# Two transformer layers with routed experts: results of the first experts stored at their tokens' places, and sums and values kept on chip

## The chip, the cores and the metric

The kernel runs on one core of a Trainium2 chip, as one program. The metric is the device time of one execution in microseconds; the number shown for a kernel is the median of its runs. All data are float32.

## The reference

Four sequences of 1024 tokens (4096 rows) of width 256 pass through four blocks, each with a layer norm in front and a residual around it. The functions, cut to what is computed:

```python
x = L0_attn_x                                   # (4, 1024, 256)
x = x + L0_attn(layernorm(x))                   # x W_in -> silu * sigmoid; A, B, C = x W_A, x W_B, x W_C (N = 16)
                                                # state = state * exp(A) + x B; out = sum(state * C); rms norm; W_out
x = x + L0_ffn(layernorm(x))                    # 8 experts, top 2 of softmax(x gate_w + gate_b)
                                                # expert e: relu(x w1[e] + b1[e]) w2[e] + b2[e], hidden 512
x = x + L1_attn(layernorm(x))                   # below
x = x + L1_ffn(layernorm(x))                    # shared: silu(x Sg) * (x Su) Sd, FS = 256
                                                # + top 2 of 16: silu(x Wg[e]) * (x Wu[e]) Wd[e], F = 128

def L1_attn(x):                                 # 16 heads of 16
    Q, K, V = split(x @ W_qkv.T)
    Q, K = rope(Q), rope(K)                     # x0 cos - x1 sin, x0 sin + x1 cos, on even and odd columns
    scores = where(causal, Q K^T / 4, -inf)
    return softmax(scores) V @ W_o.T

def L0_ffn(x):
    topk_vals, topk_idx = top_k(softmax(x @ gate_w.T + gate_b), 2)
    ...
    return sum(expert_out[topk_idx] * topk_vals)  # two rows per token, weighted
```

## The kernel before

The program is a row of six stages. Each is one block with a list of instructions per engine (SP, which issues DMAs; TensorE; VectorE; ScalarE, called ACT; GpSimd, called POOL), written out by hand, with semaphores between the lists and a barrier between stages. A tile is 128 tokens; there are 32.

**Front** (0 to 421 us): layer norm, gate, scan and output projection, then the router of the first experts, in chunks of four tiles. VectorE writes the normalised rows `r_xn` (L516), one instruction for each tile; it finds for each token and choice the expert (`best_all`, L538) and the position in that expert's region (`pos_f`, L538 to L566). GpSimd sends each tile's rows twice, by indirect stores, into `gathered_dram`, where each expert's rows lie together (L364 to L370). Behind each region lie rows of zeros, stored by SP from `zeros`. At the end VectorE works out the list of tiles to run, and `moved` (L659, L660), the distance between an expert's region and its tiles in the list.

**First experts** (421 to 697 us), `run_wide_experts`: 71 tiles from the list. For each, SP loads 128 gathered rows and the expert's first weights; TensorE turns the rows, multiplies by both weights; VectorE adds biases, ACT applies the relu and, three tiles later, stores the result at row `t * 128` of `outputs_dram` (L1406). In this stage VectorE also makes the table `pos` of places in `outputs_dram` for each token and choice (`settle`, L2733, five instructions).

**Projection** (697 to 860 us), `project_qkv`: 8 groups of 4 tiles. SP loads the rows `x1`; GpSimd fetches, with one indirect load for each tile and choice, the two expert results per token into `d_ye` (L1520 to L1526). VectorE adds them, weighted, to `x` (`add_experts`, L1561 to L1572) and takes mean and variance; GpSimd's power makes `rstd`, VectorE the bias, ACT normalises, TensorE turns the rows and multiplies by the weights: q and k transposed and split into even and odd columns, v plain. VectorE multiplies each of the four halves by the cosine or sine table, giving 8 products a group in `d_by` (`rotate`, L1601). Of the four sums of products, GpSimd makes three (`add_turned`, L1533) and VectorE the last (`last_sum`, L1589). ACT rounds each sum to a number that TensorE multiplies exactly (`hi`), VectorE takes the difference (`lo`, `rest`, L1604, L1606), and both go to `qkt_dram`, `hi` by ACT's queue and `lo` by SP's. The sum `x2` and the values `v` are stored by SP (`store_x2`, `store_v`). The work is pipelined over ticks: at tick t VectorE runs `add_experts(t)`, `rest(t-3)`, `shift(t)`, `last_sum(t-2)`, `rotate(t-1)`.

**Attention** (861 to 1361 us): 32 pairs of heads (8 pairs for each sequence). SP loads q and k for each pair, and v for each sequence (`load_v`, L1862) into `v_raw`; GpSimd spreads v into `t_vs` with a column of ones (`values`, L1924) and zeroes the masked triangle of the exponentials. The last attended pieces are copied out of PSUM by ACT (`t_att`, L1990). At step `4 * NX` of its list ACT issues the load of the second experts' up weights `wgu_sb`, 4.2 MB (`fetch(act)`, L1996; the issue is at L2794).

**Back** (1361 to 1505 us): 16 groups of two tiles. SP loads for each the attended heads, their inverse sums and the residual `x2` (`k_res`, L2189 to L2200), in a ring. VectorE scales the heads (L2276), TensorE multiplies by W_o, VectorE adds the residual (`add_res`, L2278), normalises, and routes; GpSimd sends the rows into the second `gathered_dram` by indirect stores. The down weights of the second experts and the shared ones are fetched by ACT's queue here.

**Second experts and finish** (1505 to 1712 us). In the second experts' loop GpSimd already sends the results to their tokens' places by indirect stores.

Lines of issue that the steps touch:

```python
for tick in range(groups + 2):                     # GpSimd, projection
    if live(tick + 1): gather(tick + 1, range(J // 2))
    if live(tick):     rsqrt(tick)
    if live(tick + 1): gather(tick + 1, range(J // 2, J))
    if live(tick - 2): add_turned(tick - 2, 0); add_turned(tick - 2, 1)
```

## Time and profile before

| | |
|---|---|
| median of 3 runs | 1712.64 us (1706.57 to 1714.9) |
| the profiled execution's own time | 1713.81 us |
| its span | 1712.1 us |
| TensorE busy | 1522.8 us (89%) |
| VectorE busy | 1000.7 us (58%) |
| ACT busy | 734.9 us (43%) |
| GpSimd busy | 575.6 us (34%) |
| DMA | 235.21 MB, mean 137 GB/s |
| front | 0 to 421 us |
| first experts | 421 to 697 us |
| projection | 697 to 861 us |
| attention | 861 to 1361 us |
| back | 1361 to 1505 us |
| second experts | 1505 to 1652 us |
| finish | 1652 to 1712 us |

All come from one profiled execution, but for the median. The busy shares are means over stages of quite different make-up. A stage begins with the first load of its own that SP issues behind the barrier; the bounds are read from those loads and are good to a microsecond or two.

### The profile page before, as it was taken

To read this page: it belongs to the slowest core of one execution; us is meant where nothing else is said; L and a number is where in the kernel's file an instruction comes from. 1 tells how busy PE (TensorE), PEld (TensorE's weight loads), DVE (VectorE), ACT (ScalarE), POOL (GpSimd) and SP (SyncE) were. 2 spreads that over 40 slices of the span, in tenths; PEclk is the share of its full clock that TensorE was granted. 3 is DMA by queue.
4 is the path that set the end of the run, shared out by engine and by line. 5 is a ranking of instruction groups with operands and counts; after the bars stand their busy time and mean duration, and the time that the engine had idled before them with its cause. 6 is when DMAs were issued, how large, how long until landed. Compare 5 with 4: busy or idle time off the path is not lost. (4 is left out here: it accounts for less than half of the span.)

```text
span 1712.1 us, 31150 instructions
## 1 busy us (share of the span) xinstructions
PE 1522.8 (89%) x9903; PEld 1138.2 (66%) x9903; DVE 1000.7 (58%) x3394; ACT 734.9 (43%) x1537; POOL 575.6 (34%) x1009
## 2 busy tenths in 40 slices
PE   6999999982999999588588999999999679579988
PEld 3777777762999999344365666666666468458877
DVE  3344544442332323378877888888888258645558
ACT  3444444420222222233325777776777523234420
POOL 3123333334000000478452323333222227735530
PEclk9999999985999999799889999999999979789999
DMA  7001111113777776478879767667664276755546
GB/s 224 1 25 44 47 47 47 35 50 130 223 207 218 206 216 190 148 226 293 263 115 190 99 93 116 91 92 112 94 94 69 63 227 204 188 134 156 157 154 206
DMA packets 170062, 235.21 MB, mean 137 GB/s; under 512 B 25040, under 2 KB 121936, under 8 KB 169776
## 3 DMA queue, kind: packets, MB, share of 16 engines
q1 hardware_dynamic: 134128, 171.55, 43.4%
q0 software_dynamic: 13008, 35.57, 6.3%
q10 hardware_dynamic: 22768, 26.11, 4.8%
q8 instruction: 84, 1.38, 0.3%
q14 instruction: 74, 0.61, 0.1%
HBM read 147.90 MB, written 84.98 MB: 136 GB/s over the span
## 5 line engine op out<-in xcount | busy, mean ns | idle before, releaser
L1983 ACT ACTIVATE t_probs<-t_ps_st 128x512 f32<-128x512 f32 x576 | 313.1, 596 | 134.9 <-PE t_ps_st L2037 125.4
L1964 DVE CUSTOM_DVE_ANT_0 t_seen<-t_ps_s,t_later 128x512 bf16<-128x512 f32 (+3 forms) x512 | 285.8, 587 | 22.9 <-PE t_ps_s L2023 20.8
L2037 PE MATMUL t_ps_st<-t_qs,t_ks 128*128 128x512 f32 (+3 forms) x768 | 244.0, 367 | 7.3 <-ACT t_probs L1983 5.7
L2023 PE MATMUL t_ps_s<-t_ks,t_qs 96*128 96x512 f32 (+3 forms) x768 | 248.7, 364 | 0.5 <-ACT t_neg_max L1976 0.5
L1936 POOL TENSOR_SCALAR_AFFINE_SELECT t_probs<-t_probs 128x128 f32<-128x128 f32 x512 | 137.3, 300 | 316.3 <-ACT t_probs L1983 314.6
L2037 PEld LDWEIGHTS t_ps_st<-t_qs,t_ks 128*128 128x128 f32 x768 | 137.5, 190 | 81.6 <-ACT t_probs L1983 43.7
L1964 DVE CUSTOM_DVE_ANT_0 t_seen<-t_ps_s,t_later,t_first_max 128x512 bf16<-128x512 f32 (+3 forms) x256 | 140.6, 549 | 50.7 <-PE t_ps_s L2023 50.7
L1524 POOL DMA_INDIRECT d_ye<-outputs_dram,r_pos_all x64 | 64.8, 1013 | 297.2 <-POOLq L1304 279.4
L2053 PE MATMUL t_ps_o<-t_probs,t_vs 128*17 128x256 f32 (+1 forms) x2560 | 155.7, 362 | 0.5 <-issue 0.5
L2023 PEld LDWEIGHTS t_ps_s<-t_ks,t_qs 96*128 96x128 f32 x768 | 139.4, 191 | 18.0 <-DVE t_first_max L1964 1.6
L1345 PE MATMUL m_ps_h<-m_xt,m_w_t 128*128 128x128 f32 x1136 | 140.2, 277 | 0.0
L1345 PEld LDWEIGHTS m_ps_h<-m_xt,m_w_t 128*128 128x128 f32 x1136 | 134.4, 194 | 0.1
L1353 PE MATMUL m_ps_y<-w_sb,m_ht 128*128 x568 | 134.4, 380 | 0.0
L834 PE MATMUL ps_h<-w_in,xnt 128*128 128x512 f32 x256 | 126.4, 619 | 0.6 <-ACT xnt L672 0.6
L1378 DVE TENSOR_TENSOR m_h<-m_ps_h,b_turned 128x512 f32<-128x512 f32 x71 | 49.1, 692 | 132.6 <-PE m_ps_h L1345 132.6
L1404 ACT ACTIVATE m_ht<-m_h 128x512 f32<-128x512 f32 x71 | 44.7, 629 | 160.2 <-DVE m_h L1378 160.2
L1353 PEld LDWEIGHTS m_ps_y<-w_sb,m_ht 128*128 128x128 f32 x568 | 102.5, 190 | 11.3 <-issue 0.3
L2053 PEld LDWEIGHTS t_ps_o<-t_probs,t_vs 128*17 128x17 f32 x2560 | 59.2, 97 | 72.3 <-issue 28.1
L1129 POOL DMA_INDIRECT outputs_dram<-m_y,m_place x79 | 75.8, 959 | 68.3 <-DVE m_place L1217 65.7
L355 POOL TENSOR_TENSOR xi<-xi,sig_z 128x512 f32<-128x512 f32 x32 | 40.6, 1269 | 139.0 <-ACT sig_z L684 138.9
L1157 PE MATMUL m_ps_h<-wgu_sb,m_xt 128*128 x316 | 82.4, 384 | 0.0
L368 POOL DMA_INDIRECT gathered_dram<-r_xn,pos x64 | 63.4, 991 | 54.0 <-DVE pos L565 38.6
(329 smaller groups left out, 2690.6 us busy)
## 6 DMA issues: line engine op xcount, KB each, us to landing
m_w_t<-in_w_dram SPq DMA_DIRECT2D x71, 512.0 KB, 4.1
t_qs<-qkt_dram SPq DMA_DIRECT2D x124, 128.0 KB, 5.8
t_ks<-qkt_dram SPq DMA_DIRECT2D x124, 128.0 KB, 6.0
m_x_t<-gathered_dram SPq DMA_DIRECT2D x79, 128.5 KB, 2.1
m_x_t<-gathered_dram SPq DMA_DIRECT2D x71, 128.0 KB, 3.8
outputs_dram<-m_y ACTq DMA_DIRECT2D x71, 128.0 KB, 4.0
qkt_dram<-d_hi ACTq DMA_DIRECT2D x32, 256.0 KB, 4.5
qkt_dram<-d_lo SPq DMA_DIRECT2D x32, 256.0 KB, 5.6
```

What stands on the lines that cost most here:

```text
L834: last = nc.tensor.matmul(ps_h[h][:], xnt[:, n % 2, j, :], w_in[:, j, h * DI:(h + 1) * DI], start=(j == 0), stop=(j == KD - 1))
L1129: nc.gpsimd.indirect_dma_start(out=outputs[:, :], out_offset=bass.IndirectOffsetOnAxis(ap=place[:, t:t + 1], axis=0), in_=y[:, t % RING, : ...
L1157: last = nc.tensor.matmul(ps_h[t % 2][:], xt[:, t % 2, j, :], w_up[:, j, bass.ts(expert[t], width)], start=(j == 0), stop=(j == KD - 1))
L1345: last = nc.tensor.matmul(ps_h[t % 2][:, f, :], w_t[:, t % WRING, j, f * P:(f + 1) * P], xt[:, t % 2, j, :], start=(j == 0), stop=(j == KD ...
L1353: last = nc.tensor.matmul(ps_y[t % 2][:, 0:DM], ht[:, t % 2, j, :], w_down[:, j, bass.ts(expert[t], DM)], start=(j == 0), stop=(j == block ...
L1524: nc.gpsimd.indirect_dma_start(out=ye[:, g % 2, j, i, :], out_offset=None, in_=outputs[:, :], in_offset=bass.IndirectOffsetOnAxis(ap=kept[ ...
L1936: nc.gpsimd.affine_select(out=diag, in_=diag, compare_op=ALU.is_ge, fill=0.0, base=0, pattern=[[1, P]], channel_multiplier=-1).then_inc(ma ...
L1964: nc.vector.tensor_tensor_reduce(out=seen[:, (NP * p + x) % (RS + 1), 0:keys], in0=bank_of(p, x)[:, 0:keys], in1=masks, scale=1.0, scalar= ...
L1983: nc.scalar.activation(probs[:, p % 2, i // NST, base:base + STC], ps_st[(NX * p + i) % RT][:], ACT.Exp, scale=HD ** -0.5).then_inc(exp_re ...
L2023: nc.tensor.matmul(bank_of(p, x)[:, 0:keys], q[0:MAX_ROW, head, qc * P:(qc + 1) * P], k[0:MAX_ROW, head, k0:k0 + keys], start=True, stop=T ...
L2037: last = nc.tensor.matmul(ps_st[(NX * p + i) % RT][:, col:col + width], k[:, head, kc * P:(kc + 1) * P], q[:, head, q0:q0 + width], start= ...
L2053: last = nc.tensor.matmul(ps_o[32 * g:32 * g + VR, col:col + width], vs[:, (p // PAIRS) % 2, kc, 2 * (p % PAIRS) + head, :], probs[:, p % ...
```

## The change

The rows of the first experts carry, in a 257th column, the place of their token and choice: row `2 * token + choice` of `outputs_dram`. VectorE writes each normalised row twice, once for each choice. After an expert's tile is done, GpSimd sends the result by an indirect store to these rows; rows of filling go to places behind. The projection then loads its two rows a token with a plain DMA, as one piece of 2 KB for each token, and GpSimd's gathers, the `settle` steps and the tables for it go. The sum stays in SBUF for the whole rest of the kernel (`total`); it is also stored, for the first 12 tiles, and loaded again in the back stage, since attention uses that part of `total` for buffers of its own. ACT writes v straight to `t_vs`; the store, load and spreading of v go. GpSimd makes all four sums of the rotation and two of the four differences, VectorE the other two. The load of `wgu_sb` moves from ACT's queue in attention to SP's queue in the back stage, behind the load of group 9. The diff at its core:

```diff
 front
-    r_xn = sb("r_xn", [P, 2, B4, DM])
+    r_xn = sb("r_xn", [P, 2, B4, 2, DM + 1])
+    r_token = sb("r_token", [P, C, B4, 2])
...
             def scatter(u, b):
                 if b == 0:
                     pool.wait_ge(pos_ready, u + 1)
+                    pool.wait_ge(r_placed, u + 1)
...
-                        in_=r_xn[:, u % 2, b, :], in_offset=None).then_inc(scattered[u % 2], 16)
+                        in_=r_xn[:, u % 2, b, i, :], in_offset=None).then_inc(scattered[u % 2], 16)
...
+                    nc.vector.tensor_copy(r_xn[:, r % 2, :, :, DM], r_token[:, r]).then_inc(r_placed, 1)
-                nc.vector.tensor_scalar(r_xn[:, r % 2, b, :], x1[:, r % 2, b, :], r_mean_var[:, b, 0:1],
+                nc.vector.tensor_scalar(r_xn[:, r % 2, b, :, 0:DM], x1[:, r % 2, b, :].unsqueeze(1).broadcast_to([P, 2, DM]), r_mean_var[:, b, 0:1],
...
-                nc.vector.tensor_copy(of_chunk(best_all, r), best_f[:]).then_inc(kept_ready, 1)
...
-                nc.vector.tensor_copy(of_chunk(pos_f_all, u), pos_f[:]).then_inc(kept_ready, 1)
 run_wide_experts
+        def _(pool):
+            def send(t):
+                pool.wait_ge(place_taken, t + 1)
+                pool.wait_ge(y_ready, t + 1)
+                nc.gpsimd.indirect_dma_start(out=outputs[:, :], out_offset=bass.IndirectOffsetOnAxis(ap=place[:, t:t + 1], axis=0),
+                                             in_=y[:, t % RING, :], in_offset=None).then_inc(stored[t % RING], 16)
...
+            def take_place(t):
+                dve.wait_ge(x_loaded[t % RING], 16 * (t // RING) + 16)
+                nc.vector.tensor_tensor(place[:, t:t + 1], x_t[:, t % RING, DM:DM + 1], spare[:, t:t + 1], ALU.min).then_inc(place_taken, 1)
...
             for i in range(n_list + 2):
-                late(dve, i)
                 if live(i - 1):
+                    take_place(i - 1)
                     hide(i - 1)
...
-            def store(t):
-                act.wait_ge(y_ready, t + 1)
-                act.dma_start(outputs[t * P:(t + 1) * P, :], y[:, t % RING, :]).then_inc(stored[t % RING], 16)
 project_qkv, SP
             def load(g):
                 wait(sp, x2_ready, J * (g - 1))
-                sp.dma_start(x_t[:, g % 2], rows(x_dram, g)).then_inc(x_loaded[g % 2], 16)
+                sp.dma_start(total[:, J * g:J * (g + 1), :], rows(x_dram, g)).then_inc(x_loaded[g % 2], 16)
+                sp.dma_start(ye[:, g % 2].rearrange("p j i n -> p j (i n)"),
+                             outputs[2 * g * TG:2 * (g + 1) * TG, :].rearrange("(j p i) n -> p j (i n)", p=P, i=2)).then_inc(ye_loaded[g % 2], 16)
...
-                if live(tick):
-                    store_x2(tick)
+                if tick < SPILL // J:          # SPILL = 12
+                    store_sum(tick)
...
-                if live(tick - 1):
-                    store_v(tick - 1)
 project_qkv, GpSimd
+                nc.gpsimd.tensor_tensor(qk[:, 2 * which + 1, :], by[:, s, which, 2, :], by[:, s, which, 3, :], ALU.add).then_inc(sum_ready, 1)
+            def rest_late(g):
+                for n in range(2, NB):
+                    pool.wait_ge(hi_ready, NB * g + n + 1)
+                    nc.gpsimd.tensor_tensor(lo[:, g % 2, n, :], qk[:, n, :], hi[:, g % 2, n].bitcast(FP32), ALU.subtract).then_inc(lo_late_ready, 1)
...
+            for tick in range(groups + 3):
+                if live(tick - 3):
+                    rest_late(tick - 3)
                 if live(tick):
                     rsqrt(tick)
-                if live(tick + 1):
-                    gather(tick + 1, range(J // 2, J))
 project_qkv, VectorE
                 if live(tick - 3):
-                    for n in range(NB):
+                    for n in range(2):
                         rest(tick - 3, n)
...
-                if live(tick - 2):
-                    last_sum(tick - 2)
 project_qkv, ACT
-                    nc.scalar.activation(v_t[:, g % 2, 2 * h:2 * h + 2, :], ps_v[:, 2 * h:2 * h + 2, :], ACT.Copy).then_inc(v_ready, 1)
+                    nc.scalar.activation(vs[:, g // 2, j:j + 2, :, 0:HD], ps_v[:, 2 * h:2 * h + 2, :].rearrange("p j (h d) -> p j h d", d=HD),
+                                         ACT.Copy).then_inc(v_ready, 1)
 attention
-                if tick % PAIRS == PAIRS // 2 and live(tick + PAIRS // 2):
-                    load_v(tick // PAIRS + 1)
...
-                if tick % PAIRS == PAIRS // 2 + 1 and live(tick + PAIRS // 2):
-                    values(tick // PAIRS + 1)
...
-                if step == 4 * NX:
-                    fetch(act)
+    att = total[:, 0:2 * KD, :].rearrange("p (s k) d -> p s (k d)", s=2)
+    seen = total[:, 2 * KD:2 * KD + RS + 1, :].bitcast(BF16)
 back, SP
-                sp.dma_start(res[:, s], res_dram[g * G * P:(g + 1) * G * P, :].rearrange("(j p) n -> p j n", p=P)).then_inc(x_loaded[s], 16)
+            def load_sum(i, tiles):
+                sp.dma_start(total[:, tiles, :], res_dram.rearrange("(t p) n -> p t n", p=P)[:, tiles, :]).then_inc(sum_loaded[i], 16)
             load(0)
+            load_sum(0, slice(0, 4))
             load(1)
             load(2)
+            load_sum(1, slice(4, SPILL))
...
                 load(g)
+                if g == 9:
+                    fetch_late(sp)             # load_moe1_up: wgu_sb, 4.2 MB
 back, VectorE
-                nc.vector.tensor_tensor(total[:, g * G:(g + 1) * G], res[:, g % R], ps_wo[g % 2][:], ALU.add).then_inc(x_ready, 1)
+                nc.vector.tensor_tensor(these, these, ps_wo[g % 2][:], ALU.add).then_inc(x_ready, 1)
```

## Rows read from the trace of the kernel before

**Rows 1.** Windows, core 0: stretch, length, busy (instructions) of PE, PEld, DVE, ACT, POOL, clock, DMA, GB/s.
```profile
445.00:698.00 253.00, 249.03 (x1727) 231.29 (x1725) 76.05 (x139) 67.13 (x132) 0.34 (x1) 1.00 0.70 200
698.00:860.00 162.00, 112.16 (x336) 63.44 (x336) 113.65 (x250) 54.97 (x104) 107.72 (x96) 0.83 0.78 246
764.00:780.00 16.00, 14.75 (x40) 7.89 (x40) 12.63 (x32) 6.13 (x12) 12.83 (x13) 0.84 0.96 319
860.00:1360.00 500.00, 488.29 (x4194) 318.82 (x4194) 404.70 (x1540) 333.48 (x640) 165.10 (x554) 0.99 0.65 101
1360.00:1500.00 140.00, 98.67 (x516) 81.23 (x516) 91.45 (x402) 42.25 (x74) 78.17 (x92) 0.83 0.72 200
```
**Rows 2.** Timeline, projection: start, us, engine, line, out<-in, xcount [idle before <-releaser].
```profile
733.97 7.11 PE L1711 MATMUL d_ps_qk<-d_xnt,d_w_qk 128*128 128x512 f32 x16 [0.77 <-DVE d_by L1601]
...
777.39 4.87 DVE L1601 TENSOR_TENSOR d_by<-d_ps_qk,d_turn 128x512 f32<-128x512 f32 x8
780.45 7.11 PE L1711 MATMUL d_ps_qk<-d_xnt,d_w_qk 128*128 128x512 f32 x16 [0.77 <-ACT d_xnt L1645]
785.87 1.67 DVE L1568 SCALAR_TENSOR_TENSOR d_part<-d_ye,r_prob_all,d_x 128x256 f32<-128x256 f32 x4 [3.61 <-issue]
787.39 3.62 PE L1718 MATMUL d_ps_v<-w_qkv,d_xnt 128*128 128x256 f32 x16
790.77 0.17 DVE L1581 TENSOR_SCALAR d_var_eps<-d_mean_var 128x4 f32<-128x4 f32 x1
790.85 2.51 DVE L1606 TENSOR_TENSOR d_lo<-d_qk,d_hi 128x512 f32<-128x512 f32 x4
791.02 1.43 POOL L1531 TENSOR_TENSOR d_rstd<-d_var_eps,mhalf 128x4 f32<-128x4 f32 x1 [1.06 <-DVE d_var_eps L1581]
...
830.13 8.97 PE L1711 MATMUL d_ps_qk<-d_xnt,d_w_qk 128*128 128x512 f32 x16 [0.20 <-DVE d_by L1601]
...
860.62 0.34 SPq L1736 DMA_DIRECT2D t_qs<-qkt_dram  x1
```
**Rows 3.** The tile `d_ye`: least/median/longest ns, first to last start; then its DMA.
```profile
L1524 POOL DMA_INDIRECT d_ye<-outputs_dram,r_pos_all x64: 944/958/1485, 697.7 to 812.3; - x64
...
  DMA d_ye<-outputs_dram,r_pos_all: 11.9, 2
```
**Rows 4.** The tile `d_by`: least/median/longest ns, first to last start.
```profile
L1601 DVE TENSOR_TENSOR d_by<-d_ps_qk,d_turn x64: 673/682/691, 730.2 to 841.1; 128x512 f32<-128x512 f32 x64
...
L1538 POOL TENSOR_TENSOR d_qk<-d_by x16: 1257/1282/1788, 749.3 to 846.3; 128x512 f32<-128x512 f32 x16
```
**Rows 5.** Timeline, end of the projection.
```profile
831.74 3.55 DVE L1606 TENSOR_TENSOR d_lo<-d_qk,d_hi 128x512 f32<-128x512 f32 x4
...
833.19 1.55 POOL L1538 TENSOR_TENSOR d_qk<-d_by 128x512 f32<-128x512 f32 x1 [5.03 <-DVE d_lo L1606]
```
**Rows 6.** Timeline of attention, ACT and its queue.
```profile
912.30 0.60 ACT L1990 ACTIVATE t_att<-t_ps_o 128x512 f32<-128x512 f32 x1
...
920.01 6.87 ACTq L2794 DMA_DIRECT2D wgu_sb<-in_w_gu_dram  x1
...
934.31 0.60 ACT L1990 ACTIVATE t_att<-t_ps_o 128x512 f32<-128x512 f32 x1
...
948.80 0.60 ACT L1990 ACTIVATE t_att<-t_ps_o 128x512 f32<-128x512 f32 x1
```
**Rows 7.** Windows, the stretch in which the up weights move (columns as Rows 1).
```profile
932.00:936.00 4.00, 4.00 (x36) 2.93 (x39) 3.32 (x15) 3.30 (x7) 1.87 (x7) 0.89 1.09 347
```
**Rows 8.** Timeline, back stage: SP's queue and VectorE at group 10.
```profile
1417.48 0.46 SPq L2200 DMA_DIRECT2D k_res<-x_dram  x1
...
1433.04 0.68 DVE L2276 TENSOR_TENSOR k_scaled<-k_headst,k_inv_t 128x512 f32<-128x512 f32 x1
```
**Rows 9.** Timeline, front stage, VectorE.
```profile
278.05 0.69 DVE L450 TENSOR_TENSOR xi<-ps_h,sig_a 128x512 f32<-128x512 f32 x1 [1.52 <-ACT sig_a L678]
...
390.56 1.38 DVE L516 TENSOR_SCALAR r_xn<-x,r_mean_var,r_rstd 128x256 f32<-128x256 f32 x4
```

More of the change, by code:

```diff
@@ L1266, with run_wide_experts @@
 WRING = 4
-def run_wide_experts(nc, sb, pb, sem, c, E, gathered, outputs, kept, w1_dram, b1_turned, w_down, b_down, weights, late):
+SPILL = 12
+def run_wide_experts(nc, sb, pb, sem, c, E, gathered, outputs, kept, w1_dram, b1_turned, w_down, b_down, weights):
     ident = c["ident"]
@@ L1323, in _ @@
                 fetch(t)
+        @block.gpsimd
+        def _(pool):
[4 more added lines that the diff above has]
+                                             in_=y[:, t % RING, :], in_offset=None).then_inc(stored[t % RING], 16)
+            nc.gpsimd.iota(spare[:], pattern=[[P, n_list]], base=2 * TOK, channel_multiplier=1,
+                           allow_small_or_imprecise_dtypes=True).then_inc(spare_ready, 1)
+            for t in range(n_list):
+                send(t)
+            for s in range(RING):
+                pool.wait_ge(stored[s], 16 * len(range(s, n_list, RING)))
         @block.tensor
@@ L1519, in _ @@
         def _(pool):
-            def gather(g, tiles):
-                wait(pool, x2_ready, J * (g - 1))
-                for j in tiles:
-                    for i in range(2):
-                        nc.gpsimd.indirect_dma_start(
-                            out=ye[:, g % 2, j, i, :], out_offset=None, in_=outputs[:, :],
-                            in_offset=bass.IndirectOffsetOnAxis(ap=kept["pos"][:, J * g + j, i:i + 1], axis=0)).then_inc(gathered[g % 2], 16)
             def rsqrt(g):
@@ L1637, in normalise @@
                 for j in range(J):
-                    nc.scalar.activation(xn[:, j, :], x2[:, g % 2, j, :], ACT.Identity, bias=bias[:, j:j + 1],
+                    nc.scalar.activation(xn[:, j, :], total[:, J * g + j, :], ACT.Identity, bias=bias[:, j:j + 1],
                                          scale=rstd[:, j:j + 1]).then_inc(xn_ready, 1)
@@ L2700, in build @@
                 phase(front, c, x_in, w_in, w_abc, w_out, norm_w, x1_dram, gate_w, gate_b, gathered[0], kept, E0, fetch)
-                kept.update(here=wsb("r0_here", [P, 2 * NT, E0]), steps=Chain(nc.vector, sem("r0_settled"), 5))
                 phase(run_wide_experts, c, E0, gathered[0], outputs[0], kept, w1, b1_turned, w2_sb, b2_sb,
-                      (moe0_loaded, 16 * (H0 // P + 2)), lambda dve, i: settle(dve, nc, kept, i))
+                      (moe0_loaded, 16 * (H0 // P + 2)))
+            total = whole.enter_context(nc.sbuf_tensor("whole_sum", [P, NT, DM], FP32, side="right"))
+            vs = ahead.enter_context(nc.sbuf_tensor("t_vs", [P, BATCH, TPB, NH, HD + 1], FP32, side="right"))
             q_first, k_first = (ahead.enter_context(nc.sbuf_tensor(n, [P, 2, SEQ], FP32R, side="right")) for n in ("t_qs0", "t_ks0"))
-            phase(project_qkv, c, x1_dram, outputs[0], kept, x2_dram, w_qkv, rope, qkt_dram, v_dram,
+            phase(project_qkv, c, x1_dram, outputs[0], kept, total, x2_dram, w_qkv, rope, qkt_dram, vs,
                   lambda eng: load_heads(eng, 0, q_first, k_first, qkt_dram, first_loaded))
@@ L2714, in build @@
         wsb = lambda n, s, d=FP32: whole.enter_context(nc.sbuf_tensor(n, s, d))
+        phase(attention, c, q_first, k_first, first_loaded, qkt_dram, vs, total, headst_dram, inv_dram)
+        ahead.close()
         wgu_sb = wsb("wgu_sb", [P, KD, E1 * 2 * F1])
-        phase(attention, c, q_first, k_first, first_loaded, qkt_dram, v_dram, headst_dram, inv_dram,
-              lambda eng: load_moe1_up(eng, moe1_loaded, wgu_sb, w_gu))
-        ahead.close()
         wd_sb = wsb("wd_sb", [P, F1 // P, E1 * DM])
```

189 lines of the change are left out of this document (66 added, 123 removed).

## The prediction

> **What bounds the kernel now.** I read the table of engines by stage first. The six stages are separated by barriers, so each has a limit of its own, and only what ends last in a stage counts. In the first experts TensorE is busy 249 of 253 us and in attention 488 of 500, both at full clock: there, work on other engines is free as long as it does not delay TensorE. The projection (698 to 860) is different: no engine is full (TensorE 112, VectorE 114, GpSimd 108 of 162 us), and the DMA share is 0.96 in its middle. The back stage (1360 to 1500) has no full engine either; its DMA share is 0.72 [rows 1].
>
> Then the projection's timeline, one group of four tiles [rows 2]. The matmuls of group 1 start at 733.97 and those of group 7 at 830.13: 16.0 us a group. The reader should see who waits: VectorE sits idle 3.61 us before a group's first sum (785.87), although TensorE and ACT have nothing late. The view of the tile that is gathered says why: 64 indirect loads, 0.96 us each on GpSimd [rows 3]. Eight of them a group with 0.3 us between are 10.1 us, three rotation sums at 1.28 [rows 4] are 3.8, the power 1.4: 15.3 of the 16.0. GpSimd sets the pace, with DMA close behind.
>
> **The projection after.** Out of GpSimd's list: all 64 gathers. Into it: one sum (1.28) and two differences (1.28 each) a group, so 6 x 1.28 + 1.4 = 9.1 us. Out of VectorE's: one sum and two differences. VectorE then has, from rows 2: weighting and statistics 5.1 (785.87 to 790.94); half of the four differences, 1.25, under which GpSimd's power runs until 1.6 after the variance; the bias 0.15; the rotation 4.87. Sum 11.7. TensorE has 7.11 + 3.62 = 10.7, plus about 1.5 for the turn of the next group, whose copy must precede its matmuls: 12.3. DMA: 3.5 MB a group instead of 4.5 (no v store, no x2 store after the third group), at the 319 GB/s of the middle of the stage [rows 1] 11.0, and 12.5 for the first three. So the floor is 12.3.
>
> On top comes what the moved work does to its neighbour. Four differences on VectorE take 2.51 us alone (790.85), but 3.55 when one sum of GpSimd falls among them, which itself takes 1.55 instead of 1.28 [rows 2, 5]: about 1.04 us lost an overlap. The rotation, which reads one side from PSUM, never exceeds 691 ns in 64 [rows 4]: it is not touched. GpSimd's four sums will fall beside the rotation, its two differences beside the weighting, which reads two SBUF operands. Both bounds: nothing lost (12.3, TensorE's floor) or 2 x 1.28 (14.3). I take 1.6, since the second difference should partly fall beside the statistics, which read one operand: 13.3 us a group. The Trainium skill, page "SBUF — State Buffer", section "Who interferes with whom", speaks against this part of the change: a VectorE instruction with two SBUF inputs and a GpSimd instruction that reads SBUF exclude each other, and the second waits for the first to finish. The rows agree. By the rule in full the group would take 14.3 us and the sum would be 6 us higher; by the rotation's row the four sums still cost nothing.
>
> Start: two later steps (below, 1.2 and 0.6) reach this stage, and group 1 no longer waits for gathers (11.9 us in two waits at the start [rows 3]; most of it returns as 1 MB more in front of the tables, bounds 0 and 8; I take 3). Its matmuls start at 733.97 + 1.8 - 3.0 = 732.8; group 7's at 732.8 + 6 x 13.3 = 812.6. Tail: 30.5 us before, from 830.13 to attention's first load at 860.62 [rows 2]. It keeps the rotation, sums, roundings and stores of two groups and loses the v store that stood ahead of lo stores in SP's queue and two waits of GpSimd for VectorE; 26.0 (bounds 24 and 30.5). Attention starts at 838.6: **-22.0 us**, the delays included.
>
> **Front and first experts.** The write of each normalised row twice, with its place, turns four VectorE instructions of 1.38 us together into about 2.5 (the price of 512 columns, 790.85 [rows 2]) plus a small copy; two other copies go. In the steady part the gate behind them had waited 1.52 us for ACT [rows 9], so this is hidden there; without that cover it would cost 8 x 1.2. In the stage's last turn (390.56) TensorE waits for it, and the queue of indirect stores starts that much later: **+1.2**. Rows of 1028 instead of 1024 bytes: nothing. In the first experts GpSimd sends one indirect store of 0.96 us per tile of 3.6 us, ACT loses 71 stores, VectorE gains 71 tiny instructions on an engine that is busy 76 of 253 us and sheds the settling of places: nothing, TensorE hides it [rows 1]. The last tile's store is an indirect one: between 0.3 and 1.0 later, **+0.6**. Both are in the -22.0.
>
> **Attention.** The load of the second experts' up weights leaves ACT's queue. Its second half held ACT for 6.87 us, and the pair in progress took 22.01 us (912.30 to 934.31) where the next took 14.49 [rows 6]: **-7.5**, all of it on the path. The loads of v, 32 copies and a fill on GpSimd also go; a few of TensorE's waits for the row of maxima stand behind them: **-1.3** (0 to -3).
>
> **Back.** The residual is no longer loaded per group (16 x 256 KB become 1.5 MB at the start): **-1.5** (0 to -4). Against that, the same 4.2 MB of weights are now issued by SP right behind the load of group 9, at 1417.9, and ahead of the load of group 10, which VectorE takes at 1433.04 [rows 8]. Alone the weights move at 347 GB/s [rows 7]: 12.1 us. The indirect stores, 8.4 of the stage's 28 MB, take some 0.2 of the DMA time, so 15.5 us: 1434.9 with latency; group 10's four transfers need 2.6 more: 1437.5, and VectorE and everything behind it (the sum, TensorE's next projection, the router) stands for **+4.5**. Bounds: 0 if the load passes the weights, 16 if the weights take the 29 us that a slower share gives (12.1 over 0.4 free). The Trainium skill, page "DMA: Bandwidth & Descriptors", section "Queues, rings and completion order", says SP and ACT own one ring each on every DMA engine, taken in ring order, with a change of ring only between packets; no row here shows a load queued behind such a block. By it the load cannot pass, as forecast; if it could, the sum would be 4.5 less.
>
> **Sum.** Against the profiled execution (span 1712.1, its own time 1713.8, 1.2 above the median of the runs, 1712.6): 1713.8 - 22.0 - 7.5 - 1.3 - 1.5 + 4.5 = 1686.0. The median should lie about 1 below: **1685 us**.
>
> **Rivals.**
> - *Clean.* The differences disturb nobody, TensorE's 12.3 holds, the load of group 10 hardly waits: 1685 - 6 - 4 = 1675, down to 1668. For: rotation untouched. Against: rows 5.
> - *Traffic jam in the back.* The weights take 29 us beside the scatters and SP's second issue is held as ACT's was (6.87): stall 16, 1685 + 11.5 = 1697. For: that row; against: 347 GB/s reached beside attention's loads.
> - *The gathers were only half of it.* VectorE becomes the bound with all its overlaps, DMA runs at 0.9 and the loads of 1.5 MB come late: 16.0 a group stays nearly, 15.8, so only start, tail and attention gain: 1685 + 6 x 2.5 = 1700, up to 1706. For: DMA at 0.96 already; against: 22% fewer bytes.
> - *Slower.* Every one of GpSimd's six operations blocks VectorE for its whole length, the rotation too: 11.7 + 6 x 1.43 = 20.3 a group, 1685 + 42 = 1727. It turns into a loss from 13.3 + 27.6 / 6 = 17.9 us a group. For: the 3.55; against: 64 rotations without a single slow one.
>
> **Chances.** Forecast (1677 to 1693) 0.55, clean 0.13, jam 0.12, half 0.13, slower 0.04, something else 0.03. Range 1671 to 1706. A difference of 0.5% (8.6 us) is about what a measurement of this kernel can tell from none. Faster 0.88 (all but slower and the upper end of half), same 0.07, slower 0.05.
>
> **What would show it.** Projection: matmuls of groups 1 and 7 some 80 us apart instead of 96, sums on GpSimd beside the rotation, a weighting of more than 1.7 us where a difference of GpSimd lies over it. Attention: no gap between the copies of the third and fourth pair, all pairs near 14.5. Back: one long wait of VectorE before group 10's scaling, near 4 us; the stage about 3 us longer. First experts: same length within 1 us. The forecast is wrong if the projection's group stays above 15, if the half clock comes back in attention, or if the load of group 10 waits over 10 us.

## The result and the profile after

The changed kernel takes 1698.62 us (median of 6 runs, 1693.89 to 1701.82), the kernel before 1710.79 (6 runs): ratio 0.9931, 95% interval 0.9917 to 0.9945. 12 us faster, where 27.6 were forecast (1712.6 to 1685). The profiled execution has a span of 1700.0 us, 12.1 under that of before.

A stage begins with SP's first load of its own. The forecast and what came, stage by stage:

| stage | before | after | difference | forecast |
|---|---|---|---|---|
| front | 421.6 | 422.4 | +0.8 | +1.2 |
| first experts | 275.4 | 276.3 | +1.0 | +0.6 |
| projection | 163.7 | 144.4 | -19.3 | -23.8 |
| attention | 500.3 | 490.5 | -9.8 | -8.8 |
| back | 145.8 | 158.7 | **+12.9** | +3.0 |
| second experts | 145.2 | 144.7 | -0.5 | 0 |
| finish | 60.2 | 63.1 | +2.9 | 0 |
| sum | 1712.1 | 1700.0 | -12.1 | -27.8 |

Each column is one execution. The front, which is the same program in all variants of the changed kernel, takes 416.0 to 423.4 us in their profiles, so its +0.8 says nothing; the first experts take 275.4 to 275.8 us in the profiles of the kernel before and its variants and 276.0 to 277.5 in the others.

The view of windows of the changed kernel (columns as in [rows 1]):

```profile
422.00:698.00 276.00, 267.70 (x1846) 248.74 (x1846) 84.10 (x213) 71.90 (x142) 68.10 (x71) 0.98 0.66 204
698.70:843.00 144.30, 102.72 (x336) 60.32 (x336) 107.52 (x226) 53.94 (x104) 73.27 (x57) 0.87 0.72 229
766.00:781.00 15.00, 12.76 (x43) 7.02 (x41) 14.66 (x30) 6.29 (x13) 9.65 (x9) 1.00 0.75 257
843.00:1333.00 490.00, 484.98 (x4194) 317.22 (x4194) 404.21 (x1540) 333.58 (x640) 150.76 (x521) 1.00 0.61 86
1333.00:1492.00 159.00, 102.58 (x516) 84.70 (x516) 91.90 (x402) 42.13 (x74) 78.87 (x93) 0.78 0.65 190
...
1390.00:1411.00 21.00, 15.84 (x91) 13.38 (x89) 13.86 (x62) 7.24 (x13) 14.33 (x15) 0.99 0.94 309
```

In the projection VectorE is now busy 14.66 of 15 us of the steady part, where it had 12.63 of 16 [rows 1]: it is the bound (the engine whose list is as long as the group). The first experts, with 71 indirect stores from GpSimd's list, take 1 us more. The back stage is the one that lost.

The timeline of the changed kernel's projection, a tick before GpSimd has any differences (first two rows), then a steady one, then the end:

```profile
742.07 1.66 DVE L1572 SCALAR_TENSOR_TENSOR whole_sum<-d_ye,r_prob_all,whole_sum 128x256 f32<-128x256 f32 x4
743.65 1.66 DVE L1576 SCALAR_TENSOR_TENSOR whole_sum<-d_ye,r_prob_all,whole_sum 128x256 f32<-128x256 f32 x4
...
769.96 7.11 PE L1703 MATMUL d_ps_qk<-d_xnt,d_w_qk 128*128 128x512 f32 x16 [0.76 <-DVE d_by L1598]
770.97 2.67 DVE L1572 SCALAR_TENSOR_TENSOR whole_sum<-d_ye,r_prob_all,whole_sum 128x256 f32<-128x256 f32 x4
771.93 2.83 POOL L1546 TENSOR_TENSOR d_lo<-d_qk,d_hi 128x512 f32<-128x512 f32 x2 [2.00 <-ACT d_hi L1653]
773.56 2.67 DVE L1576 SCALAR_TENSOR_TENSOR whole_sum<-d_ye,r_prob_all,whole_sum 128x256 f32<-128x256 f32 x4
779.48 1.26 POOL L1540 TENSOR_TENSOR d_qk<-d_by 128x512 f32<-128x512 f32 x1
779.53 1.22 DVE L1590 SCALAR_TENSOR_TENSOR d_bias<-d_mean_var,d_rstd 128x4 f32<-128x4 f32 x1 [0.31 <-POOL d_rstd L1533]
780.68 4.86 DVE L1598 TENSOR_TENSOR d_by<-d_ps_qk,d_turn 128x512 f32<-128x512 f32 x8
...
813.44 8.78 PE L1703 MATMUL d_ps_qk<-d_xnt,d_w_qk 128*128 128x512 f32 x16 [0.77 <-DVE d_by L1598]
832.48 1.70 POOL L1541 TENSOR_TENSOR d_qk<-d_by 128x512 f32<-128x512 f32 x1
834.14 2.48 POOL L1546 TENSOR_TENSOR d_lo<-d_qk,d_hi 128x512 f32<-128x512 f32 x2
843.07 0.33 SPq L1728 DMA_DIRECT2D t_qs<-qkt_dram  x1
```

Eight weightings take 2 x 1.66 us alone and 2 x 2.67 beside GpSimd's differences: 2.0 us lost. The bias, an instruction of 0.16 us (it was so at 716.07), takes 1.22 when GpSimd's first sum begins just ahead of it: 1.06 lost. The rotation is untouched, 4.86 us beside three of GpSimd's sums. The matmuls of groups 1 to 7 start at 732.27, 744.09, 755.92, 769.96, 784.45, 798.96 and 813.44: 11.8 us a group at first, 14.5 from the point at which the differences join.

Attention, ACT's copies (they answer to [rows 6]): every pair takes 14.5 us, the one of 22.01 is gone.

```profile
909.55 0.60 ACT L1958 ACTIVATE whole_sum<-t_ps_o 128x512 f32<-128x512 f32 x1
924.03 0.60 ACT L1958 ACTIVATE whole_sum<-t_ps_o 128x512 f32<-128x512 f32 x1
```

The back stage of the changed kernel, SP's queue, VectorE and TensorE around group 10 (it answers to [rows 8]):

```profile
1389.70 6.87 SPq L2746 DMA_DIRECT2D wgu_sb<-in_w_gu_dram  x2
1396.61 7.39 SPq L2162 DMA_DIRECT2D k_headst<-headst_dram  x1
...
1405.20 0.15 DVE L2270 SCALAR_TENSOR_TENSOR k_bias<-k_mean_var,k_rstd 128x2 f32<-128x2 f32 x1
1414.98 0.69 DVE L2247 TENSOR_TENSOR k_scaled<-k_headst,k_inv_t 128x512 f32<-128x512 f32 x1 [9.64 <-DMA k_inv_t<-inv_dram]
...
1415.73 3.78 PE L2410 MATMUL k_ps_wo<-k_w_o,k_scaled 128*128 128x256 f32 x8 [9.27 <-DVE k_scaled L2247]
...
1423.78 1.92 PE L2410 MATMUL k_ps_wo<-k_w_o,k_scaled 128*128 128x256 f32 x8
```

The window in which TensorE comes back:

```profile
1413.00:1416.00 3.00, 0.27 (x1) 0.27 (x2) 1.01 (x2) 0.00 (x0) 0.00 (x0) 0.50 0.46 155
```

And of the tile `wgu_sb`, from issue to landing:

```profile
DMA to landing us min/median/max: 14.5/18.0/21.5
```

The second half of the weights lands 21.5 us after its issue. SP is held 6.87 us by the weights and 7.39 by the first of group 10's four transfers, so the last of the four is issued only at 1407.0, when VectorE has been ready for 1.6 us; the load of group 10 is there 25 us after the weights were issued, 9.64 us after VectorE is ready for it. TensorE had nothing to do for those 9 us and comes back at half clock (1.2 GHz, granted clock 0.50): the projection of group 10 takes 3.78 us, the next 1.92.

### The profile page after: what moved, and what is told of

Read it like the earlier page. It is cut to its first block and busy times, and to the rows that moved or that the text cites. A ratio compares the mean times of both kernels' runs of the same rounds, so it can differ in the third digit from the quotient of the medians.

```text
span 1700.0 us, 31193 instructions
## 1 busy us (share of the span) xinstructions
PE 1514.9 (89%) x9903; PEld 1137.1 (67%) x9903; DVE 1001.0 (59%) x3426; ACT 734.0 (43%) x1537; POOL 595.8 (35%) x1011
## 3 DMA queue, kind: packets, MB, share of 16 engines
q8 instruction: 84, 1.38, 0.4%
## 5 line engine op out<-in xcount | busy, mean ns | idle before, releaser
L1932 DVE CUSTOM_DVE_ANT_0 whole_sum<-t_ps_s,t_later 128x512 bf16<-128x512 f32 (+3 forms) x512 | 285.7, 587 | 16.4 <-PE t_ps_s L1989 14.3
L1932 DVE CUSTOM_DVE_ANT_0 whole_sum<-t_ps_s,t_later,t_first_max 128x512 bf16<-128x512 f32 (+3 forms) x256 | 140.6, 549 | 48.0 <-PE t_ps_s L1989 48.0
L1337 POOL DMA_INDIRECT outputs_dram<-m_y,m_place x71 | 68.1, 959 | 207.5 <-DVE m_place L1410 199.8
L1375 PEld LDWEIGHTS m_ps_y<-w_sb,m_ht 128*128 128x128 f32 x568 | 102.5, 190 | 11.3 <-issue 0.3
L1132 POOL DMA_INDIRECT outputs_dram<-m_y,m_place x79 | 75.7, 958 | 67.9 <-DVE m_place L1220 64.8
```

The source lines that it names most:

```text
L1132: nc.gpsimd.indirect_dma_start(out=outputs[:, :], out_offset=bass.IndirectOffsetOnAxis(ap=place[:, t:t + 1], axis=0), in_=y[:, t % RING, : ...
L1337: nc.gpsimd.indirect_dma_start(out=outputs[:, :], out_offset=bass.IndirectOffsetOnAxis(ap=place[:, t:t + 1], axis=0), in_=y[:, t % RING, : ...
L1375: last = nc.tensor.matmul(ps_y[t % 2][:, 0:DM], ht[:, t % 2, j, :], w_down[:, j, bass.ts(expert[t], DM)], start=(j == 0), stop=(j == block ...
L1932: nc.vector.tensor_tensor_reduce(out=seen[:, (NP * p + x) % (RS + 1), 0:keys], in0=bank_of(p, x)[:, 0:keys], in1=masks, scale=1.0, scalar= ...
```

## The experiments

Four questions: what set the pace of the projection before, what GpSimd's work costs beside VectorE's, what the place of the up weights costs, and what was gained in attention. Each is a small edit to one of the two kernels. Four of the runs lay on a chip on which the kernel before took 1729.68 us: the differences on VectorE, the up weights behind the last load and on ACT's queue (both on the changed kernel), and the kernel before with the weights behind group 9. Neither kernel was profiled there, and the changed one was not run there at all; so the ratios of these four cannot be set beside 0.9931, and they are compared with each other, by stage.

### The gathers back in the projection

```diff
-                sp.dma_start(ye[:, g % 2]..., outputs[2 * g * TG:2 * (g + 1) * TG, :]...)
+            def gather(g, tiles):                     # GpSimd, halves on either side of the power
+                        nc.gpsimd.indirect_dma_start(out=ye[:, g % 2, j, i, :], in_=outputs[0:2 * TOK, :],
+                            in_offset=bass.IndirectOffsetOnAxis(ap=row_no[:, J * g + j, i:i + 1], axis=0))
```

> The changed kernel, with one part undone: in the projection GpSimd fetches the two rows of a token again by 64 indirect loads, eight a group, of the same bytes. Theory (GpSimd's list set the pace of the projection before): it now has 8 x (0.96 + 0.30) + 1.4 + 6 x 1.35 = 19.6 us a group, so the groups go from 14.5 to 19.6 and the stage from 144 to some 144 + 7 x 5.1 = 180 us; the kernel is 35 us slower than the changed one. Rival (DMA, with a share of 0.96, set it before, and fewer bytes made the gain): the bytes are those of the changed kernel, the groups stay at 14.5, the stage within 5 us.

1727.27 us, 31.3 over the changed kernel on the same chip (1695.98). The projection takes 174.8 us, 28.8 more, and the groups are 18.75 us apart; the DMA share of a steady group is 0.65. Timeline:

```profile
788.02 2.48 POOL L1553 TENSOR_TENSOR d_lo<-d_qk,d_hi 128x512 f32<-128x512 f32 x2
790.65 0.97 POOL L1533 DMA_INDIRECT d_ye<-outputs_dram,d_row_no  x1 [0.16 <-issue]
```

```profile
785.30 6.67 DVE L1586 SCALAR_TENSOR_TENSOR whole_sum<-d_ye,r_prob_all,whole_sum 128x256 f32<-128x256 f32 x4 [2.18 <-DMA d_ye<-outputs_dram,d_row_no]
```

The theory holds (it had 19.6 us a group and 180 for the stage): the same bytes, issued by GpSimd, cost 4.25 us a group. GpSimd's list sets the pace here, not DMA. In the kernel before the DMA share was 0.96 [rows 1]; that DMA alone would have allowed shorter groups there was not tested. VectorE is idle for the gathered rows (2.18 us, second fence), and its four weightings take 6.67 us beside GpSimd's sums and differences.

### The differences on VectorE

```diff
-            def rest_late(g):                          # GpSimd
-                for n in range(2, NB):
-                    nc.gpsimd.tensor_tensor(lo[:, g % 2, n, :], qk[:, n, :], hi[:, g % 2, n]..., ALU.subtract)
...
-                    for n in range(2):                 # VectorE
+                    for n in range(NB):
                         rest(tick - 3, n)
```

> The changed kernel, with all four differences of the rotation on VectorE again, as in the kernel before; GpSimd keeps its four sums. Theory (GpSimd's two differences take 2.0 us a group from VectorE's weighting beside them): the eight weightings of a group fall from 5.3 to 3.3 us, VectorE's own differences grow from 1.3 to 2.5, under which the wait for the power (0.3) also goes: a steady group of 14.5 becomes 13.4, five such groups, and the tail loses 3 us of GpSimd's chain: 1698.6 - 5.5 - 3 = 1690. Rival (the weighting is longer because it works in place on the sum kept on chip, GpSimd takes nothing): weighting stays 5.3, a group becomes 14.5 + 1.2 = 15.7, the kernel 1705.

1705.51 us, ratio to before 0.9852 (0.9824 to 0.988). Its projection takes 144.3 us, against 145.2 and 145.9 in the two runs on the same chip that kept GpSimd's differences: 1 to 2 us less, not 8. The kernel's time is the rival's 1705, but the rival's mechanism is refuted below. Timeline of a steady tick:

```profile
787.50 1.66 DVE L1565 SCALAR_TENSOR_TENSOR whole_sum<-d_ye,r_prob_all,whole_sum 128x256 f32<-128x256 f32 x4
789.08 1.66 DVE L1569 SCALAR_TENSOR_TENSOR whole_sum<-d_ye,r_prob_all,whole_sum 128x256 f32<-128x256 f32 x4
...
792.45 3.56 DVE L1596 TENSOR_TENSOR d_lo<-d_qk,d_hi 128x512 f32<-128x512 f32 x4
...
793.97 1.49 POOL L1540 TENSOR_TENSOR d_qk<-d_by 128x512 f32<-128x512 f32 x1
795.42 1.71 POOL L1541 TENSOR_TENSOR d_qk<-d_by 128x512 f32<-128x512 f32 x1
795.93 1.22 DVE L1583 SCALAR_TENSOR_TENSOR d_bias<-d_mean_var,d_rstd 128x4 f32<-128x4 f32 x1
```

Half of the theory is shown: the weightings, still in place on the sum, are at 2 x 1.66 us again, so it was GpSimd that made them longer. The other half fails, because the cost has moved: GpSimd's first sum now begins under the differences (3.56 us instead of 2.5), the second under the bias (1.22 instead of 0.16). A group is 14.4 us long. What has to be chosen is not which engine does the work, but what lies beside it.

### The sums beside the rotation alone

```diff
                 if live(tick - 2):
+                    if live(tick):
+                        pool.wait_ge(bias_ready, tick + 1)
                     add_turned(tick - 2, 0)
```

This stands on top of the edit before.

> The changed kernel with all four differences on VectorE, and GpSimd's four sums held until VectorE's bias is written, so that they lie beside the rotation, which reads one side from PSUM, and beside nothing else. Theory (each of GpSimd's instructions with two SBUF operands costs VectorE about 1 us where VectorE's own reads two as well, and nothing beside the rotation): the four differences fall from 3.56 to 2.5, the bias from 1.22 to 0.16, a steady group from 14.4 to about 12.4, TensorE's own floor; five groups, -9 us against the run with the differences on VectorE alone, stage 135. Rival (GpSimd's sums, 5.1 us, are now the longest thing behind the bias, the rounding and the stores come 2 us later and the tail grows): groups at 12.5 but the tail 3 us longer, -6.

1685.84 us, 10.1 under the changed kernel on the same chip; projection 132.9 us, where the changed kernel has 146.0 there. Timeline:

```profile
784.20 2.49 DVE L1598 TENSOR_TENSOR d_lo<-d_qk,d_hi 128x512 f32<-128x512 f32 x4
786.61 0.15 DVE L1585 SCALAR_TENSOR_TENSOR d_bias<-d_mean_var,d_rstd 128x4 f32<-128x4 f32 x1
786.68 4.87 DVE L1593 TENSOR_TENSOR d_by<-d_ps_qk,d_turn 128x512 f32<-128x512 f32 x8
...
786.84 1.28 POOL L1540 TENSOR_TENSOR d_qk<-d_by 128x512 f32<-128x512 f32 x1 [1.08 <-DVE d_bias L1585]
...
790.54 1.28 POOL L1541 TENSOR_TENSOR d_qk<-d_by 128x512 f32<-128x512 f32 x1
```

All four sums run in 5 us beside a rotation that still takes 4.87. The groups are 11.8 us apart to the end (779.86, 791.69, 803.51), as the first groups of the changed kernel were, in which VectorE had room and TensorE set the pace. Now VectorE's list is as long (window of one group, columns as in [rows 1]):

```profile
779.86:791.69 11.83, 11.44 (x41) 6.94 (x41) 11.80 (x30) 6.21 (x13) 6.24 (x5) 1.00 0.69 227
```

One added wait made the stage 11 us shorter than in the run with the differences on VectorE (on another chip), and it is 13 shorter than in the changed kernel on this one. The tail is 28.2 us.

### The up weights behind the last load

```diff
-                if g == 9:
+                if g == NG - 1:
                     fetch_late(sp)
```

Once on the changed kernel:

> The changed kernel, with the up weights of the second experts issued behind the load of group 15 instead of group 9. Theory (the load of group 10 stood behind the weights in SP's queue): VectorE's wait of 9.64 us before group 10's scaling is gone, and so is the half clock of TensorE after it (1.7 us); the weights move under the 40 us that lie between the last load and the second experts. Back stage 158.7 - 11.3 = 147.4 us, the kernel 1687 against 1698.6. Rival (4.2 MB cost their transfer time wherever they lie, since DMA is the limit of the stage): the wait moves to the stage's end, the zeros and the indirect stores land some 12 us later, the kernel stays at 1698.

1698.33 us, ratio 0.9813 (0.9787 to 0.984), on the slower chip; 1687 was expected, and the rival's number was 1698. VectorE has no long wait at group 10 (the scalings of groups 9 and 10 are 6.6 us apart instead of 16.3), and the back stage takes 163.1 us, against 167.8 in the run there with the weights behind group 9. So 4.7 of the 11.3 expected show; this profile has two other gaps, of 10 and 8 us at groups 12 and 8, with no wait for a load, where the other has one of 8. All three are groups in which TensorE worked in part at half clock: the window at group 12 (columns as in [rows 1])

```profile
1415.00:1418.00 3.00, 3.00 (x9) 2.37 (x8) 2.48 (x7) 1.55 (x3) 2.39 (x3) 0.50 0.37 112
```

has eight matmuls of 128x256 in 3.76 us, which take 1.97 at full clock, and VectorE then waits 3.87 us for TensorE. In the other two the granted clock is 0.57 over four microseconds (1386 to 1390, and 1438 to 1442 in the run with the differences on VectorE). Before the fall at group 12 TensorE had been idle 1.88 us for ACT and had been busy 2.06 of 3 us; what let it fall there, and not at the other groups, is not known.

And once on top of the sums beside the rotation, beside that run on one chip:

> As the run before it (differences on VectorE, sums beside the rotation), with the up weights issued behind the load of group 15. It stands beside the run before on the same chip, so that the place of the weights is measured alone. Theory (waiting in SP's queue behind the block): 11.3 us less in the back stage. Rival (their transfer costs wherever it lies): the difference is under 4 us. If both edits hold, this version is the fastest, some 20 us under the changed kernel.

1677.48 us against 1685.84, and its profiled execution 1668.86 against 1687.06; the back stage takes 146.2 us against 156.7. One of its four executions took 2583.63 us, far from every other time of any kernel here; the median of the other three is 1675.46. It was run again:

> The changed kernel with the differences on VectorE, the sums beside the rotation and the up weights behind the load of group 15, once more and in more rounds, since one of its four times was far off. Expected again near 0.981 of the kernel before: projection 133, back stage 146, ratio 0.978 to 0.983.

1676.09 us (1673.23 to 1676.37), ratio 0.9792 (0.9768 to 0.9816); projection 132.4, back stage 149.0. Of the 10.5 us by which the back stage is shorter, 5.0 lie between the scalings of groups 6 and 8: there the run with the weights behind group 9 has a granted clock of 0.50 from 1369 to 1380, and the weights are issued only at 1379.0. The place of the weights itself shows between the scalings of groups 9 and 11: 19.9 us with the weights behind group 9, 13.2 with them last, so 6.7 us here, with a wait for the load of only 5.34. In the changed kernel the same stretch takes 24.3 us, 11.1 more than 13.2. The scalings of groups 9 and 10 in the first of the two:

```profile
1380.27 0.69 DVE L2242 TENSOR_TENSOR k_scaled<-k_headst,k_inv_t 128x512 f32<-128x512 f32 x1
1386.85 0.68 DVE L2242 TENSOR_TENSOR k_scaled<-k_headst,k_inv_t 128x512 f32<-128x512 f32 x1
```

### The up weights on ACT's queue, at the same moment

```diff
-                if g == 9:
-                    fetch_late(sp)                     # SP
...
+                if g == 7:
+                    fetch_late(act)                    # ACT, ahead of normalise(7)
```

> The changed kernel, with the up weights issued at about the same moment of the back stage, but by ACT's queue, ahead of its work on group 7. Theory (waiting in one queue): SP's load of group 10 is issued and lands at once, VectorE's wait before its scaling falls from 9.64 to under 2 us; but ACT is held by the issue, as in attention before (6.87 us), and normalises group 7 that much later, so the kernel comes to 1698.6 - 11.3 + 6.9 = 1694. Rival (bandwidth: a transfer of 4.2 MB slows the loads beside it whatever queue they are in): the loads of groups 8 to 10 land some 10 us late as well, and ACT's hold comes on top: 1698.6 + 6.9 = 1705.

1703.72 us, ratio 0.9849 (0.9823 to 0.9875), near the rival's 1705 and not the theory's 1694; back stage 161.2 us, against 167.8 in the run with the differences on VectorE, where the weights are on SP's queue behind group 9. Timeline:

```profile
1394.48 5.01 ACTq L2746 DMA_DIRECT2D wgu_sb<-in_w_gu_dram  x2
1398.32 0.57 SPq L2162 DMA_DIRECT2D k_headst<-headst_dram  x1
1399.59 1.52 ACT L2374 ACTIVATE k_xn<-whole_sum,k_bias,k_rstd 128x512 f32<-128x512 f32 x2 [4.52 <-issue]
...
1404.80 0.69 DVE L2245 TENSOR_TENSOR k_scaled<-k_headst,k_inv_t 128x512 f32<-128x512 f32 x1
1414.76 0.69 DVE L2245 TENSOR_TENSOR k_scaled<-k_headst,k_inv_t 128x512 f32<-128x512 f32 x1 [3.17 <-DMA k_inv_t<-inv_dram]
```

With the block in the other queue, SP's issues beside it take 0.57 us again and group 10 is scaled without a wait for its load; group 11 waits 3.17 us. So most of the 9.64 us comes from the block being in SP's own queue; some 3 us remain with the block elsewhere. How much of it is SP being held by the issues (6.87 and 7.39 us) and how much the order of the transfers behind them was not separated. The price moves to ACT, held for 5 us.

### The kernel before with the weights in the back stage

```diff
-                if step == 4 * NX:                     # attention, ACT
-                    fetch(act)
...
+                if g == 9:                             # back, SP; in a second run: g == NG - 1
+                    fetch_late(sp)
```

> The kernel before, with one part of the change alone: the up weights of the second experts leave ACT's queue in attention and go to SP's in the back stage, behind the load of group 9. Theory (in attention the whole 7.5 us of the pair in progress came from ACT being held by that issue; in the back stage the same block costs 9.6 us of wait and 1.7 of half clock): attention 500.3 - 7.5 = 492.8, back 145.8 + 11.3 = 157.1, the kernel 1710.8 + 3.8 = 1714.6. Rival (attention got shorter because the loads and copies of v went): attention 500 still, the kernel 1710.8 + 11.3 = 1722.

> The kernel before, with one edit: the up weights of the second experts leave ACT's queue in attention and are issued by SP in the back stage, behind the load of group 15. Theory (ACT's hold by the issue is what the load costs in attention, and behind the last load of the back stage nothing waits for it): attention 494, as in the run with the weights behind group 9, back stage 146 as before, the kernel 6 us faster than before (ratio 0.9965). Rival (the transfer slows the indirect stores and the zeros at the stage's end): back stage 150 or more, no gain.

Behind group 9: 1733.81 us against 1729.68, ratio 1.0018 (1.0 to 1.0036): 4.1 us more, where the theory had 3.8 and the rival 11. Behind group 15: 1708.07 against 1711.52, ratio 0.9974 (0.9953 to 0.9996), 3.4 us less, where 6 were expected; the back stage takes 153.3 us in its profile, not 146, which is what the rival said. Of these 7.5 us 3.4 lie behind group 15's scaling (44.8 us to the second experts for 41.4), so the last place is not quite free; the rest lies before it and cannot come from the weights, which are issued later: at group 8 a gap of 10.1 us stands under a granted clock of 0.50. Attention took 494.3 and 498.4 us in their profiles, not 492.8: the pair of 22.01 us fell to 14.5, but the next one, in which GpSimd spreads v, grew, to 15.7 us in the one and to 17.8 in the other. ACT's copies in the other:

```profile
911.68 0.60 ACT L1990 ACTIVATE t_att<-t_ps_o 128x512 f32<-128x512 f32 x1
926.21 0.60 ACT L1990 ACTIVATE t_att<-t_ps_o 128x512 f32<-128x512 f32 x1
944.02 0.60 ACT L1990 ACTIVATE t_att<-t_ps_o 128x512 f32<-128x512 f32 x1
```

The pair of 17.8 us has a granted clock of 0.67 from 928 to 932, so part of its length is TensorE at half clock. A later pair takes 18.1 us (it ends at 1180), with 0.61 from 1164 to 1168. In the changed kernel no pair is longer than 14.6 us and the clock stays at 1.00. So of its 9.8 us in attention 1.9 to 6 come from the weights' move and the rest from v, more than the 1.3 that the prediction gave it. The theory here had the mechanism and not the split.

### The first pair's loads at the end of ACT's list

On top of the fastest version. In the projection's tail ACT issues the eight loads of attention's first pair (7 us) ahead of the rounding of group 6.

```diff
             for tick in range(groups + 2):
-                if tick == groups:
...
-                    fetch(act)
...
+            fetch(act)                                 # behind all ticks
```

> As the run before it, and the loads of attention's first pair of heads are issued by ACT at the end of its list in the projection instead of ahead of the rounding of the last two groups. Theory (the stage's tail is ACT's: it is held 7 us by those eight issues, and rounding, GpSimd's sums and the last stores stand behind them): the tail of 28.2 us falls by 4 to 24. Rival (the last stores of the low parts in SP's queue end the stage, whatever ACT does, or the first pair now lands late): stage within 1 us, attention's first matmul up to 4 us later.

1673.94 us against 1676.09, ratios 0.9787 and 0.9792: no difference. The tail is 27.6 us instead of 27.9. Group 6 is rounded from 4.0 us behind group 7's first matmul instead of 10.5, but the sums of group 7 end 17.6 us behind it instead of 18.7, since they stand beside VectorE's differences, and the stage ends 10.0 us behind them instead of 9.2:

```profile
809.97 3.55 DVE L1598 TENSOR_TENSOR d_lo<-d_qk,d_hi 128x512 f32<-128x512 f32 x4
...
812.93 1.71 POOL L1541 TENSOR_TENSOR d_qk<-d_by 128x512 f32<-128x512 f32 x1
813.67 3.19 DVE L1598 TENSOR_TENSOR d_lo<-d_qk,d_hi 128x512 f32<-128x512 f32 x2
...
816.27 1.71 POOL L1541 TENSOR_TENSOR d_qk<-d_by 128x512 f32<-128x512 f32 x1
```

The theory falls. ACT's hold is not the tail's bound. The chain of sums, rounding and differences is seen to be long; that it alone is the bound was not tested.

### The changed kernel again

> The changed kernel as it is, once more, beside the three that follow, since the runs before this one lay on a chip on which the kernel before took 1729.7 us instead of 1710.8. If the ratio carries over, it is again near 0.993; if that chip's slower back stage (small waits of VectorE and TensorE among the weights' transfer and the indirect stores) weighs on both kernels alike, the difference in microseconds is again near 12.

1695.98 us against 1710.05, ratio 0.9907 (0.9879 to 0.9935), 14 us. Back stage 161.1, finish 61.6.

## Why the prediction was wrong

Faster was right, and 1698.6 lies in the range of 1671 to 1706, but the size was not: 12 us instead of 27.6. None of the prediction's own signs of being wrong came: the groups stayed at 14.5 (15), the clock in attention at 1.00, the load of group 10 waited 9.64 us (10). Each term was wrong by less than its sign allowed, and the large errors lay in one direction. By its own steps:

**The back stage, +12.9 instead of +3.0, is two thirds of the miss.** The mechanism was right (the load of group 10 comes behind the weights, and VectorE waits before its scaling), the step that failed is the term of +4.5, which was too small. "15.5 us, 1434.9 with latency" for the 4.2 MB was worked out with a DMA free but for a share of 0.2. They took 21.5 us: between 1390 and 1411 DMA moved 309 GB/s, 6.5 MB, of which a third was not the weights. Its 347 GB/s "alone" were no price of the weights either: they are all that DMA moved in that stretch of attention [rows 7], and in the same trace the slower half of the weights lands 29.3 us after its issue. Group 10's transfers took another 3.3, and the whole came 25.3 us after the first issue, where the forecast had 19.6 and VectorE was ready at 15.6. So 9.6 us of wait for 4.5. Left out altogether was TensorE's half clock after a wait of that length (groups 10 and 11 are 7.98 us apart instead of some 6.4: 1.6 us), and the residual's gain of 1.5 came to 0.4 (the scaling of group 9 lies 65.2 us into the stage, before 65.6). The last 40 us of the stage are 2.1 longer; 1.3 of them are there when TensorE turns the last list (25.35 us behind the scaling of group 15, before 24.05), after a stretch at a granted clock of 0.53, in which the logits of a group take 1.89 us and not 1.06. The rest was not followed up. The rival "traffic jam" named the place, and its hold of SP came (6.87 and 7.39 us), but it overstated transfer and wait (29 us and 16). That its total, 1697, is nearly the measured one is luck: the back stage lost 9.9 us beside the forecast, where it had 11.5, and the projection the next 4.5. The run on ACT's queue agrees with the rule of the Trainium skill, page "DMA: Bandwidth & Descriptors", section "Queues, rings and completion order": with the block in the other engine's ring the load went through.

**The projection, -19.3 instead of -23.8.** Its three parts: the start gained 3.4 (forecast 3.0). The groups came to 13.5 us on the mean (forecast 13.3), but by another road than the one told. TensorE's floor is 11.8, not 12.3, and VectorE's own list, 14.5 less the 3.1 us that it loses, is 11.4; the first groups ran at TensorE's floor. From the fourth on a group takes 14.5, beyond the upper bound of 14.3, since the loss was not 1.6 but 3.1: the two differences take 2.0 from the weightings, and the first sum, which was to fall beside the rotation, falls beside the bias, which the prediction had at 0.15 with nothing beside it, and takes 1.06, as the fence above shows. The step that failed is "GpSimd's four sums will fall beside the rotation". The sums' place follows from what releases them, and that was the power, not the bias. Where they do lie beside the rotation, the forecast that they cost nothing held exactly. The tail was the larger error: 29.6 us for 26.0 forecast. The end of the stage behind the last difference did shrink, from 10.3 to 6.5 us, by what no longer stands in SP's queue; but from group 7's first matmul to the last sum it grew from 17.9 to 20.7, since GpSimd makes four sums in a row (5.8 us, two of them 1.7 long beside VectorE's differences) where it had three. Of a part that moves to the slower engine, the end of the stage pays the full length.

**Attention, -9.8 for -8.8,** was right in size; the split was not (-7.5 for the weights, where the two runs of the kernel before with the weights moved gave 6.0 and 1.9). **Front and first experts, +1.8 for +1.8:** the first experts are 1 us longer, as forecast; that the front's part fits is luck, since it varies by more. The write that was to grow from 1.38 to 2.5 us takes 1.91, and TensorE's last router matmuls stand 0.5 us later, not 1.2.

**Finish, +2.9 for 0.** Its code is the same. VectorE waits 7.0 us in it for stores of the result, before 4.3. In the other runs of both kernels the stage takes 59.6 to 61.7 us, so 1 to 2 us of this belong to this one execution.

That GpSimd's gathers, and not the bytes, set the pace of the projection, the chief claim of the first part, is shown by the gathers put back into the changed kernel; for the kernel before, with its greater traffic, it is the likely reading.

## What to carry to other kernels

When GpSimd shares work with VectorE, list what lies beside each of its instructions: beside a VectorE instruction that reads one side from PSUM it is free, beside one with two SBUF operands it costs about 1 us each, even if that one is a tiny one. A wait that puts it into the right place can be worth more than the work it takes over. A large load that is wanted late goes behind the last small load that is wanted soon, in the same queue; count for it the whole DMA traffic of the stretch, the hold of the issuing engine, and the half clock after the wait. The time that the same load took from issue to landing in the old trace is a better first figure than its bytes over the highest rate seen.

## What the runs showed of the hardware

A VectorE instruction of 128x4 with two SBUF operands takes 1.22 us instead of 0.16 when a GpSimd sum of 1.26 us begins ahead of it. That two such instructions exclude each other is what the Trainium skill states, page "SBUF — State Buffer", section "Who interferes with whom"; the traces agree, and show the size and that it holds for tiny operands too. The issue of one transfer of 128 KB held SP 7.39 us when 4.2 MB stood ahead of it, and 0.57 when they stood in ACT's queue. In the back stage the scalings of two groups lie mostly 6.2 to 6.6 us apart at full clock, and 8 to 10 at several groups where TensorE was granted 0.5 for part of the group, without any wait for a load. The kernel before took 1710 to 1712 us in three sets of runs and 1729.7 in the fourth, on another chip; the variant of it profiled there has a back stage of 174.3 us, where 157 was expected.
